# Softplus in a selective-scan kernel: the larger of x and ln(1 + exp(min(x, 30))), with the bound made on GpSimd

## The reference

```python
xc = silu(depthwise_conv(x_in) + b_conv)            # 512 channels
dt = jax.nn.softplus(xc @ W_dt.T + b_dt)            # the line that is changed
Bm, Cm = xc @ W_B.T, xc @ W_C.T                     # 16 states
h = exp(dt * A_n) * h + dt * xc * Bm_n              # for each of the 16 states, along time
y = sum_n h_n * Cm_n
```

## Time and profile before

| | |
|---|---|
| time, median of 3 runs | 3281.81 us (3275.70 to 3290.30) |
| the profiled execution | 3286.47 us, span 3284.6 us |
| PE busy | 2940.8 us (90%) |
| DVE busy | 2830.4 us (86%) |
| ACT busy | 2730.2 us (83%) |
| POOL busy | 2259.7 us (69%) |

### The profile page before, as it was taken

How to read it: one execution, slowest core, us unless ns; L and a number is a source line. 1 busy time by engine, 2 the same in 40 slices (tenths; PEclk the granted TensorE clock), 3 DMA queues, 4 the chain that set the end, 5 groups by cost and what they waited for, 6 DMA issues and landing times. The chain is left out here.

```text
span 3284.6 us, 53802 instructions
## 1 busy us (share of the span) xinstructions
PE 2940.8 (90%) x18754; PEld 2365.6 (72%) x18754; DVE 2830.4 (86%) x4767; ACT 2730.2 (83%) x5298; POOL 2259.7 (69%) x943
## 2 busy tenths in 40 slices
PE   6999999999999999999999999999999997566664
PEld 4777777777777777777777777777777776455453
DVE  4899999999999999999999999999999997544442
ACT  5999999999999999999999999999999996211110
POOL 1777777777767676767676776777777775377776
PEclk9999999999999999999999999999999998688887
DMA  3112221122222221212222222212222111477774
GB/s 112 59 59 69 70 67 61 63 68 70 70 70 70 61 70 61 60 63 71 70 70 71 70 70 70 70 61 70 70 71 70 61 56 33 130 147 148 148 150 79
DMA packets 196172, 252.93 MB, mean 77 GB/s; under 512 B 45664, under 2 KB 174144, under 8 KB 195904
## 3 DMA queue, kind: packets, MB, share of 16 engines
q1 hardware_dynamic: 171328, 211.73, 20.5%
q0 software_dynamic: 24576, 37.77, 7.0%
HBM read 188.36 MB, written 61.08 MB: 76 GB/s over the span
## 5 line engine op out<-in xcount | busy, mean ns | idle before, releaser
L345 POOL TENSOR_TENSOR hid<-hid,c_all 128x1536 f32<-128x1536 f32 x512 | 1768.4, 3459 | 840.7 <-DVEq L607 820.0
L612 DVE TENSOR_TENSOR_SCAN hid<-decay,hid,psB 128x1024 f32<-128x1024 f32 x512 | 1201.6, 2347 | 79.4 <-PE psB L914 31.5
L386 ACT ACTIVATE decay<-dt,a_neg 128x383 f32<-128x383 f32 x2048 | 1085.7, 604 | 0.5 <-issue 0.2
L914 PE MATMUL psB<-ident,dbu_t 128*128 128x128 f32 x6144 | 853.2, 275 | 85.6 <-DVE hid L612 61.8
L374 ACT ACTIVATE dbu_t<-dtu_t,b_t 128x512 f32<-128x512 f32 x1376 | 893.2, 710 | 5.9 <-PE psB L914 5.8
L914 PEld LDWEIGHTS psB<-ident,dbu_t 128*128 128x128 f32 x6144 | 699.9, 141 | 197.4 <-issue 84.7
L926 PE MATMUL psY<-ident,hid 128*128 128x128 f32 x6144 | 756.9, 273 | 0.0
L926 PEld LDWEIGHTS psY<-ident,hid 128*128 128x128 f32 x6144 | 689.6, 141 | 0.3
L612 DVE TENSOR_TENSOR_SCAN hid<-decay,psB 128x512 f32<-128x512 f32 x512 | 623.5, 1218 | 8.5 <-PE psB L914 5.2
L996 PE MATMUL psM<-u,w_dt 128*128 128x384 f32 x1024 | 351.5, 487 | 3.8 <-ACT u L416 3.1
L1394 ACT ACTIVATE e_sg<-e_psU 128x256 f32<-128x256 f32 x64 | 24.5, 383 | 342.3 <-PE e_psU L1436 264.1
(11 more groups left out here) (153 smaller groups left out, 3310.2 us busy)
## 6 DMA issues: line engine op xcount, KB each, us to landing
c_all<-bc_rows_dram SPq DMA_DIRECT2D x128, 768.0 KB, 4.9
out_dram<-h SPq DMA_DIRECT2D x64, 384.0 KB, 5.7
h<-out_dram SPq DMA_DIRECT2D x32, 384.0 KB, 3.5
x_weights_dram<-normed SPq DMA_DIRECT2D x32, 384.0 KB, 2.6
xt<-in_x_t_dram SPq DMA_DIRECT2D x32, 375.0 KB
xs<-in_x_dram SPq DMA_DIRECT2D x32, 256.0 KB
e_wg<-in_gate_dram SPq DMA_DIRECT2D x64, 128.0 KB
e_wu<-in_up_dram SPq DMA_DIRECT2D x64, 128.0 KB
```

The source lines that it names most:

```text
L345: nc.gpsimd.tensor_tensor(hid[k % 4][:, :, :], hid[k % 4][:, :, :], c_all[:, k, :].unsqueeze(1).to_broadcast([P, CH, L]), ALU.mult).then_i ...
L386: last = nc.scalar.activation(decay[k % 4][:, c, 1:L], dt[q][:, c, 1:L], ACT.Exp, scale=a_neg[:, c, k:k + 1])
L612: nc.vector.tensor_tensor_scan(h[:, lo:hi], flat(decay[k % 4])[:, lo:hi], flat(psB)[:, lo:hi], h[:, lo - 1:lo] if j else 0.0, ALU.mult, AL ...
L914: last = nc.tensor.transpose(flat(psB)[:, i * P:(i + 1) * P], dbu_t[k % 2][:, t, c * P:(c + 1) * P], ident[:, :])
```

## The change

ScalarE's Abs is taken out. GpSimd makes min(x, 30) of two chunks in its place (`bounded_dt`), ScalarE makes ln(1 + exp(.)) of that, and VectorE takes the larger of x and the result. Half 1 of ScalarE's part is issued one step later.

```diff
+BOUND_AT = (5, 7)
+LINEAR = 30.0
...
+            def bounded_dt(n, half):
+
+                a, z = 2 * half, 2 * half + 2
+                for name in last_of(f"D{a}", f"D{z - 1}"):
+                    pool.wait_ge(s_out[slot(name)], number(name, n))
+                after(pool, s_dt[half], n)
+                nc.gpsimd.tensor_scalar(soft[:, a:z, :], xin[:, a:z, TAPS - 1:], LINEAR, None,
+                                        ALU.min).then_inc(s_bd[half], 1)
+
+            for half in range(2):
+                bounded_dt(0, half)
             for b in range(NB):
                 for k in range(NS):
                     times_c(b, k)
                     if k + 3 in POOL_PART:
                         scaled_part(b, b % 2, k + 3)
+                    if b + 1 < NB and k in BOUND_AT:
+                        bounded_dt(b + 1, BOUND_AT.index(k))
...
             def softplus(n, half):
 
                 a, z = 2 * half, 2 * half + 2
-                for name in last_of(f"D{a}", f"D{z - 1}"):
-                    act.wait_ge(s_out[slot(name)], number(name, n))
-                nc.scalar.activation(soft[:, a:z, :], xin[:, a:z, TAPS - 1:], ACT.Abs).then_inc(s_de[half], 1)
-                act.wait_ge(s_de[half], 2 * n + 1)
-                nc.scalar.activation(soft[:, a:z, :], soft[:, a:z, :], ACT.Exp, scale=-1.0).then_inc(s_de[half], 1)
-                act.wait_ge(s_de[half], 2 * n + 2)
+                act.wait_ge(s_bd[half], n + 1)
+                nc.scalar.activation(soft[:, a:z, :], soft[:, a:z, :], ACT.Exp).then_inc(s_de[half], 1)
+                act.wait_ge(s_de[half], n + 1)
                 nc.scalar.activation(soft[:, a:z, :], soft[:, a:z, :], ACT.Ln, bias=1.0).then_inc(s_dl[half], 1)
...
                     if k == 8:
-                        if front:
-                            softplus(n, 1)
                         if early:
                             probs(a)
                     if k == 9:
                         if front:
+                            softplus(n, 1)
                             copy_b(n, r)
...
-                nc.vector.scalar_tensor_tensor(out=dt[r][:, a:z, :], in0=xin[:, a:z, TAPS - 1:], scalar=0.0,
-                                               in1=soft[:, a:z, :], op0=ALU.max, op1=ALU.add).then_inc(s_dt[half], 1)
+                nc.vector.tensor_tensor(dt[r][:, a:z, :], xin[:, a:z, TAPS - 1:], soft[:, a:z, :],
+                                        ALU.max).then_inc(s_dt[half], 1)
```

More of the change, by code:

```diff
@@ L188, in sequence_phase @@
         s_de = [sem(f"dt_exp{j}") for j in range(2)]
+        s_bd = [sem(f"dt_bounded{j}") for j in range(2)]
         s_dl = [sem(f"dt_log{j}") for j in range(2)]
```

## The result

The changed kernel takes 3450.44 us (median of 4 runs, 3444.39 to 3451.74), the kernel before 3280.01 beside it: a ratio of 1.0495, interval 1.0472 to 1.0518. It is slower by 170 us. The profiled execution took 3449.64 us (span 3447.9), 163 more than that of before. The forecast, 3411 (3385 to 3440), had the direction and the main place; it was 39 us short. The measured time lies inside the whole range of the prediction, 3370 to 3465.

The account below looks back on a forecast made before the run. VectorE, ScalarE and TensorE were nearly full at once, with a chain from VectorE's row maximum deciding. 31 x 4.39 = 136 us, less 7 for clock falls, is 129 on 3281.8: 3411 us, range 3385 to 3440.

Parts of the forecast that it names:

- Abs, and VectorE's last step: Abs off ScalarE is worth its full 1.7 us a batch only if ScalarE sets the pace; VectorE's new maximum costs nothing.
- the rival that ScalarE sets the pace: Removing Abs takes 1.7 us a batch off the whole kernel, giving 3228 us; 4 in 100.
- the forecast's own chain: From VectorE's negated row maximum through ScalarE's exponentials, decays, copies, scalings, Exp and Ln: half 1 comes 4.39 us later each batch.
- its lower bound, 3.74: The delay of half 1 per batch, in us, if TensorE is so far ahead that neither of ScalarE's copies waits.
- The grant that TensorE would be 0.57 us earlier: TensorE's B and C rows come 0.57 us earlier, its former wait for ScalarE's silu of z; without it, 4.96 a batch.
- The copy of B: ScalarE's copy, behind half 1, comes 1.8 us later, but TensorE's attention product is still ready before VectorE asks: covered.
- so it is covered: Half 0's minimum delays GpSimd's product 6 to end at 1379.2, before product 7 is due; VectorE reads no product.
- the rival in which the two engines block each other: GpSimd's later work holds up VectorE's two-input instructions in steps 8 and 9, 1.4 us a batch, giving 3454 us; 14 in 100.
- The rival's second place: Half 1's minimum ends at 1385.2 on GpSimd, making the weights' product on VectorE, due at 1384.60, 0.6 us late.
- Half a credit of 7 us: TensorE's pause at 1357.87 goes, so some of eight clock falls may go: half of 13 us taken off.
- The pause in step 10: TensorE pauses about 3 us each batch and the clock falls behind it, costing 52 us, giving 3463; 9 in 100.
- Repaid: VectorE gets the delay back from its 2.78 us idle a period, giving 3332, 10 in 100; in full, 3 in 100.

Follow-up runs that it names:

- kernel 3: The order of before, with ScalarE taking Exp of x itself, no GpSimd minimum, and VectorE taking the larger of x and the result: 3286.96 us, 1.0002 of before.
- kernels 5 and 6: The changed kernel with half 1 ahead of the three scalings (5: 3395.49 us), or right behind the row exponentials, ahead of decays and copies (6: 3322.43 us).
- kernel 1: The kernel before, with Abs and without minima, only half 1 of the softplus moved as in the changed kernel: 3466.36 us, 1.055 of before.
- kernel 4: The changed kernel with half of GpSimd's product of step 6 left out, so that it ends before VectorE's comparison: 3441.81 us, 1.0473 of before.
- kernel 9: The changed kernel with half 1 in its old place, plus GpSimd operations on idle buffers ahead of the first batch: one profiled run, 3326.79 us.
- kernel 8: The order of before without bound, minimum or VectorE's maximum; ScalarE's Ln writes dt itself: 3265.66 us, 0.995 of before.
- Kernel 2: The changed kernel with half 1 back in its old place ahead of the row exponentials; minima and maximum stay: 3320.43 us, 1.0107 of before.
- kernel 7: The changed kernel with half 1 in its old place and half of GpSimd's product of step 6 left out: 3296.23 us, 1.0045 of before.

## Why the prediction came out as it did

**Abs, and VectorE's last step.** Right: kernel 3 shows both together at no change, so the rival that ScalarE sets the pace falls.

**Half 1 moved.** Right in mechanism: the wait comes in each batch, where and behind what the forecast said, and kernels 5 and 6 show that it is the price of what stands ahead of half 1. The size in the sum was 4.39 us, and 3.80 was measured. With the negated maximum 1.28 us late, the forecast's own chain no longer waits for the copy of B and C, which is the case of its lower bound, 3.74; the wait for TensorE there, which it named as a sign, is all but gone. With the maximum on time it is 5.67 less the Abs of 0.84, 4.83 (kernel 1), and with the maximum 0.45 late 4.60 (kernel 4), both between 4.39 and 4.96. The grant that TensorE would be 0.57 us earlier was wrong. It hands over the rows of B and C 9.97 us behind the start of step 8's scan in kernel 4 and 9.93 before, and it still waits for the silu of z 28 times, 16.0 us in all, as in the kernel before (the first row, TensorE's waits in the changed kernel):

```profile
PE psM L1057 <- ACT zs_t L427: 16.0, 28, 0.6
...
PE psM L977 <- ACT b_t L457: 20.1, 31, 1.6
```

**The copy of B.** Covered, as forecast: TensorE waits for it in every batch (the second row), but step 10, in which VectorE takes up the product behind it, keeps its length.

**GpSimd's minimum.** This step failed. I took 1.3 us, between 0.836 and 1.645, because one input is read in place of two; 2.13 was measured, above both bounds. The line through products of two tensors was not an upper bound for another kind of operation, and at 768 elements it is short for the product too (1.80, kernel 9). The Trainium skill's figure (GPSIMD Engine Reference, section Elementwise — side-by-side cycle accounting), 769 ns for a loop of 512 elements in the best case, gave an estimate of 1.15 us; the trace doesn't agree, and it is the trace that counts.

What failed with it was "so it is covered". Product 6 is not read by VectorE, but VectorE's comparison has to wait while it runs. By the forecast's own 1.3 us the product ended at 1379.2, 0.5 us behind the start of the comparison at 1378.69; the sum put this at nothing, and only the rival counted it. The price of 2.13 made 1.28 of it. So the rival in which the two engines block each other, held at 14 in 100 and 3454 us, is what came: 37.5 us in step 7, against its 1.4 x 31 = 43. A longer two-input instruction in step 8 was also one of the signs by which I would be wrong. The rival's second place, the weights of step 9, did not get longer. That its 3454 is so near 3450 is luck in part: it kept the 136, of which 117.8 came, and the -7, which became +4.0.

**The two do not add up as costs to be saved.** Seen from the old order, the late comparison costs 1.29 a batch (85.78 - 84.49) and the move 3.89 more (89.67 - 85.78). Seen from the changed kernel, removing the late comparison gives back 0.27 (kernel 4): 0.80 goes into the longer wait, since the chain through the row maximum has TensorE's projection as a second limit close behind it, and 0.30 is lost in step 8.

**The clock.** Half a credit of 7 us was wrong, for the pause that should have gone stayed: 7 of the 31 periods still last 1.3 to 1.6 us longer than 89.67, six of them with a clock fall in step 4. The pause in step 10 came as the rival said (3.10 us), and the clock falls behind it, but step 11 is only 4.0 us longer in all and not 52. This fits the rival's own "against it", that VectorE has two scan pieces to do before it needs TensorE; no kernel tried it by itself.

**Repaid.** No: none of the steps 10 to 15 is shorter by more than 0.7 us over the 31 periods.

**The sum.** 136 became 117.8, nothing became 37.5 for the late comparison, -7 became +4.0, and nothing became 5.7 ahead of the first scan. Of these, 2.6 are not the change's. TensorE's first projections of dt took 5.49 us at a granted clock of 0.50, where they had taken 2.85 at 1.00 (windows, before and changed, columns as above):

```profile
39.79:42.64 2.85, 2.85 (x8) 1.44 (x8) 0.00 (x0) 1.25 (x1) 0.00 (x0) 1.00 0.00 0
```

```profile
39.97:45.46 5.49, 5.49 (x8) 2.52 (x8) 0.00 (x0) 1.25 (x1) 0.00 (x0) 0.50 0.00 0
```

They took 5.49 us in kernel 8 as well, which has neither the minima nor the move. From ScalarE's bias behind them to the first scan, 24.31 us became 27.16. There the first batch's minima stand on the path with nothing to cover them: ScalarE's first Exp waits 2.27 us for GpSimd. Kernel 2, with the minima and the old order, needs 27.21, and kernel 1, with the move and Abs, 28.46; so either alone makes a delay of this size.

## What to carry to other kernels

Moving a step later in a queue costs what is ahead of it now, less the reserve its reader had: walk the chain from the last thing that it waits for, and check the second limit close behind each wait before adding costs up. An operation given to an idle engine is not free when it delays that engine's next instruction into one of a busy engine that has to wait for it. Work taken off an engine that does not set the pace bought nothing here, however full it looked.

## What the runs showed of the hardware

- On GpSimd an operation with a constant (minimum or product) took 2.12 to 2.15 us for 128x768 in float32, the product of two tensors 1.80.
- A comparison with two SBUF inputs that began under a GpSimd product did not run until the product was nearly over: 1.64 us from 1462.91, of which 0.36 are its own, so its work began at 1464.19, 0.15 before the product's end. That agrees with the rule of the Trainium skill (SBUF — State Buffer, section Who interferes with whom) that the later of the two waits for the other.
- Under the minimum it is not the whole instruction that blocks. In the changed kernel 27 weights (two inputs, the second a broadcast) lie inside a minimum, begun 1.09 us into it, and their line (the first row below; ns, min/median/max) is as before. The small operation on the sums ahead of them has one tensor input and took 0.17 before. Begun 0.55 into the minimum in the changed kernel and 0.25 into it in kernel 7 (the other rows below, VectorE's of the changed kernel, then GpSimd's and VectorE's of another batch of kernel 7), it ended 0.84 into it both times. In kernel 7 weights begun 0.34 into it ended 1.04 into it, so their own 0.36 began 0.68 into it; the negated maximum (own time 0.17), begun 1.54 into it, ended at its end. That GpSimd holds VectorE up only in stretches of the minimum is my reading of these rows; it was not measured by itself.

```profile
L829 DVE SCALAR_TENSOR_TENSOR weight<-score,winv x32: 357/358/360, 387.7 to 2971.0; 128x192 f32<-128x192 f32 x32
```

```profile
1469.68 0.29 DVE L824 TENSOR_SCALAR wsum<-wsum 128x3 f32<-128x3 f32 x1
```

```profile
1306.62 2.13 POOL L368 TENSOR_SCALAR soft<-xin 128x768 f32<-128x768 f32 x1 [0.40 <-issue]
```

```profile
1306.87 0.59 DVE L826 TENSOR_SCALAR wsum<-wsum 128x3 f32<-128x3 f32 x1
```
